# Spreading the split of the down weights over units 3 to 41, one operand per half unit

## The reference

```python
xn = layernorm(x)                     # no weights
# S4 branch: a kernel K of length 1024 from 64 complex poles (Cauchy sums, inverse FFT),
# then a causal convolution of every row with K, plus D * xn
# FFN branch: hidden 1024, inner 2752, all three matrices int4 with scale and zero per group of 64
w = (nibble - zero) * scale
h = silu(xn @ Wg.T) * (xn @ Wu.T)     # 2048 x 2752
ffn = h @ Wd.T                        # 2048 x 1024
```

## Time and profile before

| | |
|---|---|
| median of 3 executions | 1499.83 us |
| the profiled execution's own time | 1495.27 us |
| its span, first to last instruction | 1493.5 us |
| TensorE busy | 1333.8 us (89%) |
| VectorE busy | 957.6 us (64%) |
| GpSimd busy | 674.7 us (45%) |
| ScalarE busy | 457.3 us (31%) |

### The profile page before, as it was taken

One profiled execution on the slowest core, in us unless ns is written; L12 is line 12 of the kernel. 1 busy time (PEld: TensorE's weight loads), 2 busy tenths in 40 slices (PEclk: granted clock), 3 DMA queues, 4 the chain that ended last, 5 costly groups with the idle time before them and its releaser, 6 DMA issues. The chain is left out here.

```text
span 1493.5 us, 17048 instructions
## 1 busy us (share of the span) xinstructions
PE 1333.8 (89%) x6299; PEld 630.9 (42%) x6299; DVE 957.6 (64%) x1057; ACT 457.3 (31%) x801; POOL 674.7 (45%) x484
## 2 busy tenths in 40 slices
PE   1557899988998999989999999449999999999998
PEld 1423444433443444434444444124444444444444
DVE  4744478899999898678898988535233332432341
ACT  3533444434444354444444543221000000000000
POOL 3642466766678688687978786341000000000000
PEclk9978999999999999999999999769999999999999
DMA  5301554343433344344444443779756236335431
GB/s 177 86 29 70 225 166 131 125 133 115 132 124 117 131 134 140 124 139 134 142 134 141 139 137 112 233 247 365 248 185 222 92 109 221 92 110 196 126 101 57
DMA packets 164646, 218.09 MB, mean 146 GB/s; under 512 B 41426, under 2 KB 121940, under 8 KB 162644
## 3 DMA queue, kind: packets, MB, share of 16 engines
q1 hardware_dynamic: 163988, 209.86, 42.8%
q10 hardware_dynamic: 576, 7.14, 1.4%
HBM read 139.64 MB, written 77.34 MB: 145 GB/s over the span
## 5 line engine op out<-in xcount | busy, mean ns | idle before, releaser
L1310 PE MATMUL px<-xo,wo 128*128 128x512 f16 x2016 | 473.9, 389 | 59.1 <-ACT py L960 30.2
L1310 PEld LDWEIGHTS px<-xo,wo 128*128 128x128 f16 x2016 | 200.1, 100 | 308.7 <-issue 26.5
L684 POOL TENSOR_TENSOR wo<-wf,wo 128x512 f16<-128x512 f32 x147 | 236.5, 1619 | 71.9 <-ACT wo L918 71.9
L703 POOL TENSOR_TENSOR hs<-hf,hs 128x512 f16<-128x512 f32 x154 | 210.8, 1375 | 103.2 <-ACT hs L953 96.1
L1394 PE MATMUL px<-wd,hr 128*128 128x512 f16 x1056 | 235.0, 382 | 10.7 <-DMA wd<-w_d 10.7
L1310 PE MATMUL pz<-xo,wo 128*128 128x512 f16 x1008 | 233.6, 382 | 0.0
L1394 PEld LDWEIGHTS px<-wd,hr 128*128 128x128 f16 x1056 | 102.6, 98 | 131.1 <-DMA wd<-w_d 11.2
L1310 PEld LDWEIGHTS pz<-xo,wo 128*128 128x128 f16 x1008 | 99.5, 99 | 120.8 <-issue 4.6
L1925 DVE SCALAR_TENSOR_TENSOR acc<-px,acc 128x512 f32<-128x512 f32 x32 | 22.1, 691 | 155.3 <-PE px L1394 151.3
L953 ACT ACTIVATE hs<-hf 128x512 f16<-128x512 f32 x154 | 94.5, 621 | 80.8 <-DVE hf L1569 48.2
L693 POOL TENSOR_TENSOR ds<-wf,ds 128x512 f16<-128x512 f32 x69 | 104.2, 1511 | 33.1 <-ACT ds_more L939 20.1
(11 more groups left out here) (211 smaller groups left out, 1406.5 us busy)
## 6 DMA issues: line engine op xcount, KB each, us to landing
h_d<-hs SPq DMA_DIRECT2D x154, 256.0 KB, 3.7
hr<-h_d SPq DMA_DIRECT2D x56, 704.0 KB, 4.2
w_d<-ds SPq DMA_DIRECT2D x69, 256.0 KB, 3.9
wd<-w_d SPq DMA_DIRECT2D x4, 2816.0 KB, 12.5
sz<-in_sz_gate SPq DMA_DIRECT2D x21, 512.0 KB
sz<-in_sz_up SPq DMA_DIRECT2D x21, 512.0 KB
sz<-in_sz_down SPq DMA_DIRECT2D x20, 512.0 KB
xc_d<-xo SPq DMA_DIRECT2D x8, 1024.0 KB, 10.5
```

The source lines that it names most:

```text
L684: pool.tensor_tensor(w_dest(t, j, 1), w_place_of(j), w_dest(t, j, 0), ALU.subtract).then_inc(wlo_done, 1)
L703: pool.tensor_tensor(hs[:, j, :, 1, :], h_place_of(p, j), hs[:, j, :, 0, :], ALU.subtract)\
L1310: done = pe.matmul(bank[:, :], wo[t % 2][:, j, wp, k * P:(k + 1) * P], xo[p][:, j, xp, k, :], start=(j in (0, 3) and k == 0 and wp == 0 an ...
```

## The change

A half step t = 2(n-3)+i stands for half i of unit n. Step t splits one down operand (t from 0 to 76, so units 3 to 41), all in `D_ORDER`. A group takes seven half steps (3.5 units), so its two slabs and its sums fall now into even, now into odd units. The tail group is the last instead of the last but one. All splits use three slots in rotation. The order of the slabs comes from `_slabs()`, and SyncE loads slab m+2 where slab m is dequantized. `up_nibble` moves on ScalarE from behind `snap_s1` to behind `snap_u2`. At the end the wd operands are loaded whole: 0, 5 and 6 by SyncE, 1 and 2 by ScalarE behind `silu_tail(41)`, 3 and 4 during and behind unit 43. wd 0 takes the place of wf.

```diff
+def split_step(n, i):
+    return 2 * (n - 3) + i
+def half_steps(t):
+    if t % 7 == 5:
+        return [(t // 7 + 1, 0)] if t // 7 + 1 <= NG else []
+    if t % 7 == 0:
+        return [(t // 7, 1)] if t // 7 <= NG else []
+    return []
-        ds = at("ds", [P, 2, 2, 512], f16, W0 + 28 * K1)
+        ds = [at(f"ds{i}", [P, 2, 512], f16, (W0 + 28 * K1, W0 + 30 * K1, H0)[i]) for i in range(3)]
-        ds_more = at("ds_more", [P, 4, 2, 512], f16, W0 + 52 * K1)
-        w_place = [X0, X0 + 22 * K1, X0 + 56 * K1, X0 + 78 * K1, W0, W0 + 22 * K1, H0 + 20 * K1]
+        w_place = [W0, X0, X0 + 22 * K1, X0 + 56 * K1, X0 + 78 * K1, W0 + 22 * K1, H0 + 20 * K1]
# SyncE
+            def down_step(n, i):
+                t = split_step(n, i)
+                for g, h in half_steps(t):
+                    load(down_slab(g, 0, h) + 2)
+                    if g == NG:
+                        load(down_slab(g, 1, h) + 2)
+                if 1 <= t <= SPLITS:
+                    store_w((t - 1) // 7, D_ORDER[(t - 1) % 7])
+            load(slab_gate(2) + 2)
+            down_step(2, 0)
             store_h(0, 0, A11)
             store_h(0, 0, S3)
...
+                load(slab_gate(2 * g + 2) + 2)
+                down_step(n + 2, 0)
                 store_h(g, 1, A11)
-                load_down(g - 1, 1)
-                store_w(g - 1, B21)
-                load_gate(2 * g + 3)
+                load(slab_up(2 * g + 2) + 2)
+                down_step(n + 2, 1)
                 store_h(g, 1, S3)
# ScalarE
+            def down_step(n, i):
+                t = split_step(n, i)
+                for g, h in half_steps(t):
+                    if g < NG:
+                        down_nibble(g, h)
+                if 0 <= t < SPLITS:
+                    d_high(t // 7, D_ORDER[t % 7])
...
                 snap_s1(n + 2)
-                up_nibble(2 * g + 2)
+                down_step(n + 2, 0)
                 w_high(2 * g + 2, B11)
                 snap_s5(n + 2)
                 w_high(2 * g + 2, B21)
-                d_high(g - 1, B21)
                 snap_u2(n + 2)
+                up_nibble(2 * g + 2)
                 silu_first(n + 2)
+                down_step(n + 2, 1)
                 snap_u3(n + 2)
# VectorE
+            def down_step(n, i):
+                t = split_step(n, i)
+                for g, h in half_steps(t):
+                    down_words(g, h)
+                if t % 7 == 1 and 0 <= t // 7 <= NG:
+                    d_sum(t // 7, T1)
+                    d_sum(t // 7, T3)
+                if t % 7 == 3 and 0 <= t // 7 <= NG:
+                    d_sum(t // 7, T2)
+                    d_sum(t // 7, T4)
...
                 gate(2 * g + 2)
+                down_step(n + 2, 0)
                 up(2 * g + 2)
# end of phase A, SyncE
+            sp.wait_ge(wlo_done, 7 * 21 + 3)
+            load_wd(0)
+            for j in (A12, A22, S1, S2, S4):
+                store_h(NG, 0, j)
+            sp.wait_ge(prod_done, products_before(42))
+            load_hr(0, 0, 0)
+            load_hr(0, 0, 1)
# end of phase A, ScalarE
             silu_tail(41)
-            load_wd(0)
...
+            load_wd(1)
+            load_wd(2)
```

More of the change, by code:

```diff
@@ L84, with _slabs, down_slab, slab_arrived @@
 PHASE_A = products_before(NU)
+def split_step(n, i):
[6 more added lines that the diff above has]
+    return []
+def _slabs():
+    order = [("gate", 0), ("up", 0), ("gate", 1), ("up", 1)]
+    for n in range(2, 42):
+        if n == 2 or (n >= 4 and n % 2 == 0 and n < 40):
+            order.append(("gate", n // 2 + 1))
+        if n == 40:
+            order.append(("gate", 21))
+        for i in range(2):
+            if i == 1 and n >= 4 and n % 2 == 0 and n < 40:
+                order.append(("up", n // 2 + 1))
+            if i == 0 and n == 3:
+                order.append(("up", 2))
+            for g, h in half_steps(split_step(n, i)):
+                order += [("down", g, h)] if g < NG else [("tail", 0, h), ("tail", 1, h)]
+    return order
+SLABS = _slabs()
+SLAB = {s: m for m, s in enumerate(SLABS)}
+NIBBLES = [sum(s[0] != "tail" for s in SLABS[:m + 1]) for m in range(len(SLABS))]
 def slab_gate(t):
-    return 2 * t if t <= 2 else 6 * ((t - 1) // 2) + (0 if t % 2 else 3)
+    return SLAB["gate", t]
 def slab_up(t):
[L93 to L101, removed]
+    return SLAB["up", t]
+def down_slab(g, kh, half):
+    return SLAB["down", g, half] if g < NG else SLAB["tail", kh, half]
+def slab_arrived(m):
+    return sum(64 if s[:2] == ("tail", 0) else 32 for s in SLABS[m % 2:m + 1:2])
 def split_place(g, j):
-    return 7 * g + D_POS[j] if g < NG - 1 else (70 if g == NG - 1 else 63) + LAST_POS[j]
+    return 7 * g + D_POS[j]
 def sum_place(g, j):
[L111 to L131, removed]
+    return 4 * g + T_POS[j]
+SPLITS = 7 * (NG + 1)
 def conv_pieces(sp_, i):
@@ L601, in _ @@
                     .then_inc(kshift_in, 16)
-            load_wd(2, KC - 2, KC)
+            sp.wait_ge(prod_done, PHASE_A)
+            load_hr(0, 1, 0)
             sp.wait_ge(xc_out, 16 * 8)
             load_xc(0, 0, 0)
+            load_hr(0, 1, 1)
+            sp.wait_ge(hf_done, 88)
+            for i in range(3):
+                sp.wait_ge(ds_out[i], 16 * ((SPLITS - 1 - i) // 3 + 1))
+            load_acc(0, 0)
+            load_acc(0, 1)
+            for j in L_ORDER[:2]:
+                store_h(NG, 1, j)
             load_hr(0, 2, 0)
@@ L1123, in _ @@
                 snap_u2(n)
+                up_nibble(2 * g + 1)
                 silu_first(n)
[L1125 to L1126 removed]
+                down_step(n, 1)
                 snap_u3(n)
```

356 lines of the change are left out of this document (141 added, 215 removed).

## The result

The changed kernel takes 1545.65 us (median of 4 runs, 1541.8 to 1546.8) against 1498.51 for the kernel before: ratio 1.031 [1.028, 1.033], 47 us slower where 22.7 us less were forecast. (The first profile of one experiment, `a_splits`, fell into an execution at a granted clock of 0.56 throughout; it was profiled once more as `a_splits2`.)

The account below looks back on a forecast made before the run. TensorE was taken to bound late phase A, VectorE the S4 stretch. Terms -47.2 - 13.7 + 26.2 + 6 + 6 = -22.7 us took the profiled 1495.27 to 1472.6, median 1477; range 1452 to 1500.

Parts of the forecast that it names:

- Three slabs close together: Even units with down beside gate and up: third slab lands late, last product waits for snap_u3; +26.2 us, bounds 0 to 40.
- the upper bound of 40: Upper bound of the three-slab term, in us, if each new gap also brings a slow group.
- The gap of every fourth unit: Waits for snap_u2 in units 22 to 38 go, with up_nibble behind snap_u2 and up slabs issued earlier; -13.7 us.
- Nothing waits then: Claim that up_nibble behind snap_u2 and earlier up slabs leave no wait at the gaps of every fourth unit; -13.7 us.
- S4 stretch: Units 8 to 19: 24 splits instead of 21, VectorE the bound at 98 of 100 us; +6 us, bounds -3 and 16.
- Start: up(2) issued behind the xc_d stores, so product 2 of unit 3 starts 4.5 us late; +6 us, bounds 0 and 12.
- End of phase A: Changeover to phase B: waits on leftover down weights and the slow clock behind them go; -47.2 us, or 33 if wd 0 late.
- the second rival: Changeover keeps a wait: wd 0 comes late, sharing DMA engines with wd 1 and 2; +14 us, 1491; chance 0.15.
- some 2 for the hr tiles: Part of the 14 us wait kept at the changeover if wd 0 is late: some 2 us for hr tiles.
- The new gaps don't come: Three-slab units: the third slab lands within 5 us and nothing waits for it; 1451 us; chance 0.2.
- VectorE becomes the bound: All phase A: GpSimd's extra splits stretch VectorE's instructions, 38 us slower in 24 units; 1515 us; chance 0.1.
- my first rival: The third slab lands within 5 us; 768 KB needs 2 us at the changeover's rate; 1451 us; chance 0.2.

Follow-up runs that it names:

- a_splits: The changed kernel without its down slabs (no loads, nibbles or dequantizes of them; splits, sums and stores kept): 1453.9 us; profiled again in one run of 1453.6.
- a_late: The changed kernel with ScalarE's nibble of the third slab in even three-slab units moved behind snap_u3: 1527.3 us, ratio 1.020 to before.
- a_notail: The changed kernel without the four tail slabs of units 37 and 38, transfers and dequantizes: 1527.4 us, ratio 1.020 to before.
- b_up: The kernel before with only up_nibble moved on ScalarE from behind snap_s1 to behind snap_u2: 1490.2 us, ratio 0.994.
- a_xc: The changed kernel with the eight xc_d stores taken out of unit 2 and spread over later units: 1536.5 us, ratio 1.024 to before.
- a_best: Changed kernel, nibble waiting for words alone, third nibble behind snap_u3, xc_d stores spread, wd loads reordered, five down slabs a half unit later: 1505.8 us.
- the better version: The kernel before with up_nibble behind snap_u2 and the nibble waiting for the slab's words alone: 1478.5 us, ratio 0.988.
- a_wd: The changed kernel with the loads of wd 2, 3 and 4 issued on ScalarE behind its last split of h: 1541.4 us, ratio 1.029 to before.

## Why the prediction was wrong, point by point

By stretches, from the two profiles. The terms of the forecast are laid on the units that they name; unit 6 has 3.0 of the 26.2. (Unit 2 itself starts 1.6 us earlier, which makes it +51.0 for the profiled executions.)

| stretch | forecast, us | measured, us |
|---|---|---|
| units 2 to 5, the start | +6 | +18.7 |
| unit 6, three slabs | +3.0 | +10.8 |
| units 7 to 19, S4 work | +6 | +13.2 |
| units 20 to 40, -13.7 + 23.2 | +9.5 | +42.7 |
| from unit 41 on, phase B too | -47.2 | -32.8 |

*Three slabs close together, +26.2: the step that failed.* The mechanism is there in every forecast unit, but the sum was made at one place, the last product of the unit. For the seven units named, that place alone measures 23.6 us idle, close to 26.2. What the term left out: (1) the slow groups behind each gap, 16.6 us at all the gaps before last products, which I had only in the upper bound of 40; (2) VectorE waits for the same slab, and ScalarE's splits of its tiles and of h wait behind it or behind stores, and with them `snap_s1` and `snap_u2` of this and the next unit: 13.7 us idle before product 2 in units 20 to 40, where before had none (3.51 in unit 25, 10.14 in unit 38), and 7.9 before product 4; `a_late` shows that taking ScalarE out of the third slab leaves these; (3) the third slab of unit 6 takes 11.4 us, not 9.2, and the stores behind slabs 6.8 and 8.8 instead of 3.7 and 3.9; (4) the tails, 18.3 us (`a_notail`) for 7.0. In unit 6 and units 20 to 40 the forecast with this term is 41 us short, of 75 in all, and with the slabs out TensorE has no gap in late phase A. Which part of the rest of phase A (20 us short at the start and in the S4 stretch) is of slabs was not taken apart.

*The gap of every fourth unit, -13.7.* Right alone (9.0 in `b_up`), half lost in the change: TensorE's idle time for `snap_u2` in units 20 to 40 is 12.3 us before and 7.9 after, in units 20, 25, 32 and 39 instead of 22, 25, 26, 30, 34 and 38. (Over the whole kernel it is 22.7 and 23.8, but 11.0 of the latter lie in units 2 to 4.) "Nothing waits then" was wrong where VectorE stands before a slab.

*S4 stretch, +6, VectorE at 98.* The working was wrong: VectorE fell to 91.08, it waited for slabs. From the start of unit 7 to that of unit 20 (257.0 to 526.3 before, 284.8 to 567.3 after) it is 13.2 us more, and not for more work of VectorE: in units 8 to 19 it is busy 241.6 us before and 240.7 after. Without slabs the stretch is 3.1 us longer than before's.

*Start, +6.* The gap that I named, unit 3 before product 2, is there: 3.04 us for 4.5. But two gaps before product 4 (4.16 in unit 2, 5.22 in unit 3) and one of 1.64 in unit 4 were put at nothing, and the start is 18.7 us longer, over the upper bound of 12. The cause, the `xc_d` stores, is worth 9.2 of it (`a_xc`).

*End of phase A, -47.2.* Measured -32.8 (30.3 + 2.5), by a near relative of the second rival: 13.2 us and 2.1 of slow clock, where it had 14. Late is not wd 0 but the hr tiles behind the wd loads. I had counted them ("some 2 for the hr tiles") as bytes and not as the last ones in the queue, and left out wd 3 and the issue instructions that stand still.

*The rivals.* "The new gaps don't come": false. "VectorE becomes the bound": the sign and the size (1515) were nearer than mine, but the cause is false: VectorE has more room than before. That slabs cost by where they stand should have been a rival by itself: 39.4 us of difference (91.8 - 52.4) come from the slabs' places, with the same slabs in both kernels.

The Trainium skill ("DMA: Bandwidth & Descriptors", section "Anatomy of one DMA — SWDGE (gpsimd) path") gives a fit for GpSimd-issued DMAs of 2 us and the bytes at 436 GB/s. By that, an estimate, 768 KB take 3.8 us as one DMA, in line with my first rival, and 5.8 as the two that they are. These slabs, issued by SyncE, took 9.2 to 14.9 us; the measurement decides.

*Open.* `a_best` is still 7.5 us above before. Gaps in the S4 stretch (13.6 us idle for s4w) and in units 38 and 39 (10.0 and 3.1) are left in it; which slab order would take them out was not tried, nor a third slab buffer, nor a load of scales that all 16 DMA engines serve.

## What to carry to other kernels

A late transfer behind a double buffer is paid at every engine that waits for it and at every consumer behind these, not at the one gap that the profile shows first: before spreading work evenly, check whether it puts a third transfer between two that already use both buffers. Let each engine wait only for the bytes it reads: one semaphore more gave 22 us here and 11.7 in the better version, with no work moved. Look at the DMA share while one load is under way alone: 0.28 says that most engines have no part of it. A load moved out of a crowded stretch of DMA makes the next one late, so cost such an edit by the last transfer in the queue.

## What the runs showed of the hardware

The issue of a DMA by SyncE is not always free: 0.3 to 0.6 us as a rule, 3.47 for a 256 KB store in unit 38 (DMA share 0.78 from 936 to 942 us), 12.13 for an `h_d` store and 9.79 for an hr tile in the changeover (share 1.02 from 1022 to 1037, 0.99 from 1053 to 1063). With wd 2 out of the way (`a_wd`) the longest of the five `h_d` stores there stands 3.95. Everything behind it on SyncE waits as long.

One instruction of VectorE has two durations in the same unit 6 (dequantize, line L1469), and GpSimd's rows of that time say when which:

```profile
264.97 2.06 DVE L1469 SCALAR_TENSOR_TENSOR wf<-wf,sz 128x1024 f32<-128x1024 f32 x1
...
272.66 1.23 DVE L1469 SCALAR_TENSOR_TENSOR wf<-wf,sz 128x1024 f32<-128x1024 f32 x1
```

```profile
263.82 2.13 POOL L695 TENSOR_TENSOR ds<-wf,ds 128x512 f16<-128x512 f32 x1
...
279.79 1.75 POOL L695 TENSOR_TENSOR ds<-wf,ds 128x512 f16<-128x512 f32 x1 [9.74 <-ACT ds L936]
```

Beside a split of GpSimd it takes 2.06 us, with GpSimd idle 1.23. Over all 63 of this instruction in the trace of after, the 16 with GpSimd idle throughout take 1.22 or 1.23 us, the 26 with GpSimd busy throughout 2.06 to 2.18; before has 16 and 28 of the same two durations. No run took this apart; it is read from the traces alone.
